# Moving GpSimd's low-part subtraction ahead of four row scatters, and holding two of the scatters until VectorE has divided

## The chip, the cores and the metric

The kernel runs on one core of a Trainium2 chip. The metric is the device time of one execution in microseconds (us), the median of several runs. The profile is of one execution, taken by the hardware profiler, with its own time beside it.

## What is computed

One transformer block in float32 on 4 sequences of 2048 tokens, 256 wide: a linear attention of 16 heads (cosformer), a layer norm, a mixture of 8 experts with 2 chosen for each token, a second layer norm.

```python
q, k = relu(x @ Wq.T + bq), relu(x @ Wk.T + bk);  v = x @ Wv.T + bv
q_ = concat([q * sin, q * cos]);  k_ = concat([k * sin, k * cos])      # by place in the sequence
kv = einsum('nld,nlm->ndm', k_, v)
z = 1.0 / maximum(einsum('nld,nd->nl', q_, k_.sum(axis=1)), EPS)
attn = einsum('nld,ndm->nlm', q_, kv) * z[:, :, None]
x = layernorm(x + attn @ Wo.T + bo)
topv, topi = top_k(x @ router_w.T, 2);  w = softmax(topv)
out = sum over the 2 chosen experts e of  w * (gelu(x @ w1[e].T) @ w2[e].T)
x = layernorm(x + out)
```

## The kernel before

The 8192 tokens are cut into 32 pairs of 128-token tiles (`NPAIR = 32`, 8 pairs to a sequence, `PB = 8`). Products are made in a reduced-precision format with both operands split into a high and a low part: ScalarE casts a pair's x to its high part (`xs<-xraw`, L823), and another engine subtracts it from x to give the low part (`x_low`). Up to pair 10 VectorE does that subtraction (L1028), from pair 11 on GpSimd does (`XLO_POOL = 11`, L1576).

There are two stages. In the first (to about 325 us) every engine runs a program of its own with a step for each pair, called `rep` in the code; the function `pipeline` writes some steps out and puts others in hardware loops. In step `rep`, keys, values and queries are made for pair `rep`, while attention is computed for the pair `LAG = 9` before it (`j = rep - 9`), the output projection and row statistics for `j - 1`, routing for `j - 2`, and the scatter of finished rows for `j - 3`. So the scatters start in step 12. In the second stage the experts run in 135 steps over gathered blocks of 128 rows, and the remaining pairs' attention is spread between them.

Every engine works through its own instructions in program order; semaphores tie them together. The order written out in the code is the order on the engine. What matters here, in step `rep`:

- VectorE: add the sine part of attention for the first tile (L1047), choose two experts for `j - 2` (`choose`: L1108 to L1125; L1115 compares and L1125 multiplies by the deviation, both from two inputs in SBUF), place columns (L1038), add the sine part of the second tile (L1047), then `normalise_attention`: clip the denominators (`den`, L1054, 128x32), reciprocal (L1056), multiply (L1058, which counts `at_ready`). Then the residual of `j - 1` (L1150), the sum of logits (L1091), the low part of a query (L1185), the gates of `j - 2` (up to L1141), the statistics of `j - 1` (the last is `mv`, L1164) and the low part of attention. In steps 16 and 24 `state_out` and `state_split` for a sequence that ended come in as well, `state_out` ahead of `choose`.
- GpSimd: four scatters of finished rows, each an indirect DMA (L1586, `expert_rows<-rows,idx`), `x_low` for pair `rep + 1` between the second and the third, then `half_deviation` (L1617 to L1622), which turns `mv` of `j - 1` into the scale and shift that ScalarE's `normalise` (L860) and VectorE's L1125 use in the next step.
- TensorE: among others, the rank products (L641, which wait for `choose` and for both L1047), the query products (L613), then the transposes of attention (L600), which wait for `at_ready` and for the logits' sum L1091 of this step, since that frees their bank.
- ScalarE: the cosine part (`tcos`, L831) ahead of each L1047, the high part of x (L823), `normalise` (L860), which writes into `rows` and so waits for the four scatters of the step before to have landed.
- SyncE: issues the loads; the load of the next x waits for `x_low` (L429), and the first gather of the second stage (L458) waits for the scatters of the first 20 pairs, the last four of which are those of step 31.

`hold(pool)` is a no-operation that stands behind waits.

Of the kernel before, what the change touches and what calls it, by code (L numbers as in the profile page):

```python
# [42 lines left out]
NPAIR = T // PAIR  # L43
# [65 lines left out]
def build(nc, x, xT, WqT, bq, WkT, bk, WvT, bv, WoT, Wo, bo, bo_columns, rwT, w1T, w2T, consts, out):  # L109
# [4 lines left out]
    with ctx:  # L114
# [3 lines left out]
        def sem(name):  # L118
            return ctx.enter_context(nc.semaphore(name))
# [168 lines left out]
        comb_step, at_ready, tlo_ready, qlo_ready = sem("comb_step"), sem("at_ready"), sem("tlo_ready"), sem("qlo_ready")  # L288
# [13 lines left out]
        XLO_POOL = PB + 3  # L302
# [40 lines left out]
        def hook(s):  # L343

            d, n = divmod(s - FIRST_GROUP, GROUP)
            return (GROUP_PAIRS + d, n) if FIRST_GROUP <= s < LAST_GROUP else (None, s - LAST_GROUP)
# [20 lines left out]
        def hold(eng):  # L367


            eng.nop(nofuse=True)  # L370

        def parts(rep):


            return (LAG <= rep, LAG < rep, LAG + 1 < rep, rep % PB == 0 and PB <= rep, PB <= rep)

        def lagged(u, rep):

            slot = (rep - LAG) % 2
            return u * 2 + (rep % 2 - LAG), u + (rep % 2 - LAG - slot) // 2  # L380
# [1177 lines left out]
        def _(pool):  # L1558
# [14 lines left out]
            def x_low(i, rep):  # L1573
                pool.wait_ge(xhi_ready, i + 1)
                hold(pool)
                nc.gpsimd.tensor_tensor(xs[:, rep % 2, 1], xraw[:, rep % 2], xs[:, rep % 2, 0].bitcast(F32), ALU.subtract)\  # L1576
                    .then_inc(xlo_late, 1)

            def scattered(jj):
                pool.wait_ge(pos_step, (jj + 1) * POS)  # L1580
                pool.wait_ge(route_step, (jj + 1) * ROUTE)
                pool.wait_ge(x1_ready, jj + 1)
                hold(pool)

            def scatter(slot, h, k):
                nc.gpsimd.indirect_dma_start(ex, bass.IndirectOffsetOnAxis(ap=idx[:, slot, h, k:k + 1], axis=0),  # L1586
                                             rows[:, slot, h, k, :], None).then_inc(s_rows[slot], 16)
# [12 lines left out]
            def weight_half(n):  # L1600

                e, kind = n // 2, n % 2
                pool.wait_ge(s_wraw[kind], e * 16 + 16)
                c0 = kind * HALF
                w_hi, w_lo = (w[:, e, part, c0:c0 + HALF] for part in range(2))
                nc.gpsimd.tensor_copy(w_hi, wraw[:, kind]).then_inc(wprep, 1)
                pool.wait_ge(wprep, 2 * n + 1)
                for c in range(0, HALF, D):
                    a = nc.gpsimd.tensor_tensor(w_lo[:, c:c + D], wraw[:, kind, c:c + D], w_hi[:, c:c + D].bitcast(F32),
                                                ALU.subtract)  # L1610
                a.then_inc(wprep, 1)

            def half_deviation(j):

                pool.wait_ge(norm_step, j * NORM + NORM_MV)
                hold(pool)
                nc.gpsimd.tensor_scalar(vare[:], mv[:, :, 1], 4.0, 4.0 * LN_EPS, ALU.mult, ALU.add).then_inc(pow_step, 1)  # L1617
                nc.gpsimd.tensor_scalar(shift1[:], mv[:, :, 0], -1.0, None, ALU.mult).then_inc(pow_step, 1)
                pool.wait_ge(pow_step, j * POW + 2)
                nc.gpsimd.tensor_tensor(rstd[:], vare[:], half_neg[:, 0:2], ALU.pow).then_inc(pow_step, 1)  # L1620
                pool.wait_ge(pow_step, j * POW + 3)
                nc.gpsimd.tensor_tensor(shift1[:], shift1[:], rstd[:], ALU.mult).then_inc(pow_step, 1)  # L1622

            def step(u, rep):
                attn, onward, route, _, _ = parts(rep)
                par = rep % 2
                i = u * 2 + par
                j, _ = lagged(u, rep)
                slot = (rep - LAG) % 2
                scatters = rep > LAG + 2  # L1630
                if scatters:
                    scattered(j - 3)
                    scatter(1 - slot, 0, 0)
                    scatter(1 - slot, 0, 1)
                if XLO_POOL <= rep + 1 < NPAIR:
                    x_low(i + 1, rep + 1)
                if scatters:
                    scatter(1 - slot, 1, 0)
                    scatter(1 - slot, 1, 1)
                if onward:  # L1640
                    half_deviation(j - 1)
                if rep == LAST_HALF_AT:
                    weight_half(HALVES - 1)
                if rep == NPAIR - 1:
                    late_weight()
                    scattered(j - 2)
                    for h in range(2):
                        for k in range(TOPK):
                            scatter(slot, h, k)

            pool.wait_ge(proj_low, 5)
            for n in range(HALVES - 1):
                weight_half(n)
            pipeline(pool, step, begin=PB, unrolled=PB)


# [27 lines left out]
            for s in range(STEPS):  # L1684
# [4 lines left out]
                j, n = hook(s)  # L1689
# [68 lines left out]
```

## Time and profile before

| | |
|---|---|
| median of 3 runs | 869.43 us (869.2 to 871.21) |
| the profiled execution's own time | 865.97 us |
| its span, first to last instruction | 864.2 us |
| granted TensorE clock, mean | 0.980 |
| busy: TensorE / VectorE / ScalarE / GpSimd | 800.2 (93%) / 576.6 (67%) / 460.9 (53%) / 424.9 (49%) us |
| steps 12 to 30 | about 104 to 306 us |

The span lies 1.8 us below the execution's time and 5.2 us below the median of the runs. Steps of the first stage are some 10 to 11 us long. Shares of busy time are averages over both stages; what a change in the first stage brings must be read from the waits of that stage.

### The profile page before, as it was taken

Reading aid. Unit: us, or ns where it says so; the run is one execution under the profiler, and the core shown is the slowest. Engines: PE = TensorE matmul, PEld = TensorE weight load, DVE = VectorE, ACT = ScalarE, POOL = GpSimd, SP = SyncE. Lnnn points to the kernel's source line nnn. Section 1 sums busy time; section 2 is a strip of 40 time slices with the busy share of each in tenths; the row PEclk is TensorE's granted clock in tenths of the full one; section 3 lists DMA queues with packets and bytes.
Section 4 is the critical chain, followed back from the end, with each engine's and each line's share of the span. In section 5 each row is a group of like instructions: output and inputs, shape, how many; then the busy total and the mean of one; then the engine's idle time right before and its main releaser. Section 6 shows DMA issues by size and latency. Waiting matters only on the chain.

```text
span 864.2 us, 22025 instructions
## 1 busy us (share of the span) xinstructions
PE 800.2 (93%) x6684; PEld 735.2 (85%) x6684; DVE 576.6 (67%) x1816; ACT 460.9 (53%) x1044; POOL 424.9 (49%) x545
## 2 busy tenths in 40 slices
PE   4998998999989976999999999999999999999990
PEld 4888988888889865999999999998999999999980
DVE  3335888888878885677666667665444467777773
ACT  4565766666667644444455444443444445656653
POOL 3885566566656654544454445453322224444442
PEclk9999999999999997999999999999999999999995
DMA  6453133233323324323333332232422255666644
GB/s 201 155 167 102 42 102 112 75 104 105 110 75 108 113 84 123 113 83 100 104 101 95 104 94 82 84 114 80 125 75 86 83 212 196 221 228 221 220 166 171
DMA packets 56468, 106.64 MB, mean 123 GB/s; under 512 B 9261, under 2 KB 37551, under 8 KB 54448
## 3 DMA queue, kind: packets, MB, share of 16 engines
q1 hardware_dynamic: 41296, 63.25, 24.7%
q0 software_dynamic: 12624, 33.84, 10.7%
q10 hardware_dynamic: 2448, 8.26, 2.6%
q8 instruction: 58, 0.95, 0.5%
q14 instruction: 42, 0.34, 0.1%
HBM read 61.91 MB, written 44.32 MB: 123 GB/s over the span
## 4 chain that ended last, share of the span: by engine, by line
PE 77%; DVE 10%; ACT 4%; issue 4%; DMA 2%; SPq 1%; DVEq 0%; POOL 0%; ACTq 0%; POOLq 0%
PE PS L736 22%; PE PS L724 22%; PE PS L540 11%; PE PS L754 7%; PE PS L577 4%; PE PS L713 3%; DVE den L1054 2%; PE PS L629 2%; PE PS L613 2%; PE PS L600 2%; DVE o L1047 1%; ACT tcos L831 1%; DVE xtok L1150 1%; DMA xraw<-in_xT 1%; ACT vs L851 1%
## 5 line engine op out<-in xcount | busy, mean ns | idle before, releaser
L1669 POOL DMA_INDIRECT token_rows<-xg x135 | 134.8, 998 | 280.5 <-DVE xg L1403 255.2
L736 PEld LDWEIGHTS PS<-w,hT 128*128 128x128 f32 x1620 | 211.6, 189 | 12.0 <-issue 1.8
L724 PE MATMUL PS<-w,xgT 128*128 x810 | 221.8, 409 | 0.0
L736 PE MATMUL PS<-w,hT 128*128 x1620 | 217.3, 283 | 0.8 <-ACT hT L994 0.8
L724 PEld LDWEIGHTS PS<-w,xgT 128*128 128x128 f32 x810 | 143.0, 190 | 24.2
L994 ACT ACTIVATE hT<-PS 128x512 fp32r<-128x512 f32 x135 | 80.8, 598 | 135.3 <-PE PS L754 135.3
L1586 POOL DMA_INDIRECT expert_rows<-rows,idx x128 | 126.9, 991 | 44.6 <-issue 32.9
L990 ACT ACTIVATE hg<-PS 128x512 f32<-128x512 f32 x135 | 80.6, 597 | 121.2 <-PE PS L724 120.9
L1468 DVE TENSOR_TENSOR hT<-PS,hT 128x512 fp32r<-128x512 f32 x135 | 93.4, 692 | 75.2 <-ACT hT L994 75.2
L1395 DVE TENSOR_TENSOR xgT<-PS,xgT 128x256 fp32r<-128x256 f32 x135 | 57.0, 422 | 78.2 <-ACT xgT L960 77.0
L754 PE MATMUL PS<-cst,hg 128*128 128x128 f32 x540 | 81.0, 272 | 0.7 <-ACT hg L990 0.7
L540 PE MATMUL PS<-wk,xs 128*128 128x264 f32 x384 | 65.4, 307 | 13.8 <-DVE wv L1333 8.3
L1403 DVE SCALAR_TENSOR_TENSOR xg<-PS,xg 128x256 f32<-128x256 f32 x135 | 65.1, 482 | 14.0 <-PE PS L736 4.5
L540 PEld LDWEIGHTS PS<-wk,xs 128*128 128x128 f32 x384 | 52.1, 195 | 21.2 <-ACT vs L851 10.0
L577 PE MATMUL PS<-sts,qs 128*128 128x272 f32 x384 | 62.1, 298 | 7.1 <-DVE o L1047 2.4
L754 PEld LDWEIGHTS PS<-cst,hg 128*128 128x128 f32 x540 | 62.6, 140 | 1.4 <-ACT hg L990 1.4
L577 PEld LDWEIGHTS PS<-sts,qs 128*128 128x128 f32 x384 | 52.3, 192 | 9.0 <-issue 5.7
L713 PE MATMUL PS<-cst,xg 128*128 128x128 f32 x270 | 52.3, 276 | 6.4 <-DMA xg<-expert_rows 5.3
L613 PE MATMUL PS<-xs,wq 128*128 128x256 f32 x384 | 57.5, 296 | 0.0
L540 PE MATMUL PS<-wv,xs 128*128 128x256 f32 x384 | 57.1, 286 | 0.0
L629 PE MATMUL PS<-wo,aT 128*128 128x264 f32 x384 | 56.7, 286 | 0.0
L1047 DVE SCALAR_TENSOR_TENSOR o<-PS,cst,tcos 128x272 f32<-128x272 f32 x64 | 32.0, 501 | 30.9 <-ACT tcos L831 30.7
(179 smaller groups left out, 1302.1 us busy)
## 6 DMA issues: line engine op xcount, KB each, us to landing
xg<-expert_rows SPq DMA_DIRECT2D x135, 130.0 KB, 2.1
z<-token_rows SPq DMA_DIRECT2D x15, 1024.0 KB, 7.4
xraw<-in_xT SPq DMA_DIRECT2D x32, 256.0 KB, 3.3
xtok<-in_x SPq DMA_DIRECT2D x32, 256.0 KB, 3.1
out_y<-z ACTq DMA_DIRECT2D x15, 512.0 KB, 3.6
wraw<-in_w1T SPq DMA_DIRECT2D x7, 512.0 KB, 3.7
wraw<-in_w2T SPq DMA_DIRECT2D x7, 512.0 KB, 3.8
token_rows<-xg POOLq DMA_INDIRECT x135, 2.8
```

The lines of the kernel that those rows point to most:

```text
L540: return nc.tensor.matmul(PS[:, bank, 0:columns], xs[:, rep % 2, a, k, h * P:(h + 1) * P], weights[:, b, k, :], start=(n == 0), stop=(n == ...
L577: mm = nc.tensor.matmul(PS[:, bN + half, 0:2 * NW], qs[:, a, half, h * P:(h + 1) * P], sts[:, b, half].rearrange("p a b -> p (a b)"), star ...
L613: mm = nc.tensor.matmul(PS[:, bQ, half * PAIR:(half + 1) * PAIR], wq[:, a, k, half * P:(half + 1) * P], xs[:, rep % 2, b, k, :], start=(n ...
L713: mm = nc.tensor.transpose(PS[:, gX, k * P:(k + 1) * P], xg[:, XG_SLOTS[s % NXG], k * P:(k + 1) * P], ident)
L724: mm = nc.tensor.matmul(PS[:, gH, :], xgT[:, s % 2, a, k, :], w[:, bass.ds(e, 1), b, k * F:(k + 1) * F].rearrange("p o f -> p (o f)"), sta ...
L736: return nc.tensor.matmul(PS[:, gY, 0:D], hT[:, a, k, :], w[:, bass.ds(e, 1), b, HALF + k * D:HALF + (k + 1) * D] .rearrange("p o f -> p ( ...
L754: mm = nc.tensor.transpose(PS[:, gT, k * P:(k + 1) * P], hg[:, k * P:(k + 1) * P], ident)
L990: nc.scalar.activation(hg[:], PS[:, gH, :], ACT.Gelu, scale=2.0).then_inc(gelu_ready, 1)
L994: nc.scalar.activation(hT[:, 0].rearrange("p k t -> p (k t)"), PS[:, gT, :], ACT.Copy)\
L1468: nc.vector.tensor_tensor(hT[:, 1].rearrange("p k t -> p (k t)"), PS[:, gT, :], hT[:, 0].rearrange("p k t -> p (k t)").bitcast(F32), ALU.s ...
L1586: nc.gpsimd.indirect_dma_start(ex, bass.IndirectOffsetOnAxis(ap=idx[:, slot, h, k:k + 1], axis=0), rows[:, slot, h, k, :], None).then_inc( ...
L1669: nc.gpsimd.indirect_dma_start(yd, bass.IndirectOffsetOnAxis(ap=xg[:, XG_SLOTS[s % NXG], C_DST:C_GATE].bitcast(U32), axis=0), xg[:, XG_SLO ...
```

## The change

In GpSimd's step, `x_low` is moved ahead of the waits and the four scatters, and the third scatter gets a wait of its own: for `at_ready` of the step's own pair `j`, that is for VectorE's L1058 in the same step.

```diff
                 scatters = rep > LAG + 2
+                if XLO_POOL <= rep + 1 < NPAIR:
+                    x_low(i + 1, rep + 1)
                 if scatters:
                     scattered(j - 3)
                     scatter(1 - slot, 0, 0)
                     scatter(1 - slot, 0, 1)
-                if XLO_POOL <= rep + 1 < NPAIR:
-                    x_low(i + 1, rep + 1)
-                if scatters:
+                    pool.wait_ge(at_ready, j + 1)
+                    hold(pool)
                     scatter(1 - slot, 1, 0)
                     scatter(1 - slot, 1, 1)
```

The instructions of TensorE, VectorE, ScalarE and SyncE keep their order. On GpSimd, step 30 of the kernel before reads so (L1586 are scatters, L1576 is `x_low`, the rest `half_deviation`):

```order
L1586 DMA expert_rows<-rows,idx 66688x260 [waits x1_ready,pos_step,route_step]
L1586 DMA expert_rows<-rows,idx 66688x260
L1576 TENSOR_TENSOR xs<-xraw,xs 128x512 [waits xhi_ready]
L1586 DMA expert_rows<-rows,idx 66688x260 x2
L1617 TENSOR_SCALAR vare<-mv 128x2 [waits norm_step]
L1618 TENSOR_SCALAR shift<-mv 128x2
L1620 TENSOR_TENSOR rstd<-vare,half_neg 128x2 [waits pow_step]
L1622 TENSOR_TENSOR shift<-shift,rstd 128x2 [waits pow_step]
```

The same step of the changed kernel:

```order
L1576 TENSOR_TENSOR xs<-xraw,xs 128x512 [waits xhi_ready]
L1586 DMA expert_rows<-rows,idx 66688x260 [waits x1_ready,pos_step,route_step]
L1586 DMA expert_rows<-rows,idx 66688x260
L1586 DMA expert_rows<-rows,idx 66688x260 [waits at_ready]
L1586 DMA expert_rows<-rows,idx 66688x260
L1617 TENSOR_SCALAR vare<-mv 128x2 [waits norm_step]
L1618 TENSOR_SCALAR shift<-mv 128x2
L1620 TENSOR_TENSOR rstd<-vare,half_neg 128x2 [waits pow_step]
```

The subtraction has moved in front of the first two scatters, and the third scatter now waits for `at_ready`. It is the same in steps 12 to 30. Step 31 has no `x_low`; before, its four scatters run through:

```order
L1586 DMA expert_rows<-rows,idx 66688x260 [waits x1_ready,pos_step,route_step]
L1586 DMA expert_rows<-rows,idx 66688x260 x3
L1617 TENSOR_SCALAR vare<-mv 128x2 [waits norm_step]
L1618 TENSOR_SCALAR shift<-mv 128x2
L1620 TENSOR_TENSOR rstd<-vare,half_neg 128x2 [waits pow_step]
```

In the changed kernel the second half of them has the wait too:

```order
L1586 DMA expert_rows<-rows,idx 66688x260 [waits x1_ready,pos_step,route_step]
L1586 DMA expert_rows<-rows,idx 66688x260
L1586 DMA expert_rows<-rows,idx 66688x260 [waits at_ready]
L1586 DMA expert_rows<-rows,idx 66688x260
L1617 TENSOR_SCALAR vare<-mv 128x2 [waits norm_step]
```

Only the wait is new there; nothing is moved.

## Rows read from the trace of the kernel before

**Rows 1.** The page's chain that ended last, by line

```profile
PE PS L736 22%; PE PS L724 22%; PE PS L540 11%; PE PS L754 7%; PE PS L577 4%; PE PS L713 3%; DVE den L1054 2%; PE PS L629 2%; PE PS L613 2%; PE PS L600 2%; DVE o L1047 1%; ACT tcos L831 1%; DVE xtok L1150 1%; DMA xraw<-in_xT 1%; ACT vs L851 1%
```

**Rows 2.** TensorE's waits, 104 to 306 us: total us, times, longest

```profile
PE PS L600 <- DVE lsum L1091: 8.3, 15, 1.0
PE PS L641 <- DVE o L1047: 3.0, 2, 1.5
PE PS L691 <- DVE rows L1141: 0.6, 1, 0.6
```

**Rows 3.** Timeline of steps 26 and 27: start, duration, engine, line [idle before]

```profile
260.26 0.87 DVE L1054 TENSOR_SCALAR den<-o 128x32 f32<-128x32 f32 x1
...
266.72 0.66 ACT L823 ACTIVATE xs<-xraw 128x512 fp32r<-128x512 f32 x1
...
268.05 0.19 DVE L1115 TENSOR_TENSOR oh<-cst,ix 128x32 f32<-128x32 f32 x1
...
268.66 0.16 DVE L1125 TENSOR_TENSOR dls<-dl,rstd 128x2 f32<-128x2 f32 x1
...
269.14 0.49 ACT L831 ACTIVATE tcos<-PS,cst 128x272 f32<-128x272 f32 x1 [0.36 <-PE PS L577]
...
269.66 0.50 DVE L1047 SCALAR_TENSOR_TENSOR o<-PS,cst,tcos 128x272 f32<-128x272 f32 x1 [0.75 <-ACT tcos L831]
...
270.07 1.31 POOL L1576 TENSOR_TENSOR xs<-xraw,xs 128x512 fp32r<-128x512 f32 x1
...
270.20 1.23 DVE L1054 TENSOR_SCALAR den<-o 128x32 f32<-128x32 f32 x1
...
271.85 0.69 DVE L1058 TENSOR_TENSOR o<-o,den 128x512 f32<-128x512 f32 x1
...
272.84 0.96 POOL L1586 DMA_INDIRECT expert_rows<-rows,idx  x1 [0.30 <-issue]
...
273.38 0.63 PE L600 MATMUL PS<-cst,o 128*128 128x128 f32 x4 [0.39 <-DVE lsum L1091]
...
275.83 0.23 POOL L1617 TENSOR_SCALAR vare<-mv 128x2 f32<-128x2 f32 x1 [2.03 <-DVE mv L1164]
...
277.55 1.54 ACT L860 ACTIVATE rows<-xtok,shift,rstd 128x512 f32<-128x512 f32 x2
```

**Rows 4.** VectorE's L1054, grouped: 104 to 306 us, then 330 to 550 us

```profile
L1054 DVE TENSOR_SCALAR den<-o 128x32 f32<-128x32 f32 x19 | 20.9, 1098 | 0.7
...
L1054 DVE TENSOR_SCALAR den<-o 128x32 f32<-128x32 f32 x9 | 1.6, 181 | 0.3
```

**Rows 5.** Timeline of step 24, where state_out comes ahead of choose

```profile
235.72 1.79 DVE L1125 TENSOR_TENSOR dls<-dl,rstd 128x2 f32<-128x2 f32 x1
...
236.19 1.29 POOL L1576 TENSOR_TENSOR xs<-xraw,xs 128x512 fp32r<-128x512 f32 x1
...
237.65 0.98 POOL L1586 DMA_INDIRECT expert_rows<-rows,idx  x1 [0.17 <-issue]
...
238.03 0.18 DVE L1054 TENSOR_SCALAR den<-o 128x32 f32<-128x32 f32 x1
```

**Rows 6.** Busy time in two steps: length, PE, PEld, DVE, ACT, POOL, clock

```profile
258.73:268.66 9.93, 9.77 (x109) 9.12 (x108) 8.22 (x34) 6.98 (x19) 6.49 (x9) 1.00 0.36 109
268.66:278.98 10.32, 9.82 (x109) 9.15 (x108) 8.57 (x35) 6.99 (x19) 6.57 (x10) 1.00 0.33 104
```

**Rows 7.** The scatters, 104 to 306 us: durations in ns, and us to landing

```profile
L1586 POOL DMA_INDIRECT expert_rows<-rows,idx x76: 956/985/1223, 104.7 to 304.0; - x76
...
DMA to landing us min/median/max: 2.4/2.9/4.7
```

**Rows 8.** Timeline of step 31 and the first gather of stage two

```profile
314.67 0.69 DVE L1058 TENSOR_TENSOR o<-o,den 128x512 f32<-128x512 f32 x1
...
318.82 0.24 POOL L1617 TENSOR_SCALAR vare<-mv 128x2 f32<-128x2 f32 x1 [4.65 <-DVE mv L1164]
...
324.08 17.16 SPq L458 DMA_DIRECT2D xg<-expert_rows  x6
```

## The prediction, made before the changed kernel had run

> **What bounds the kernel now.** I read the page first. TensorE is busy for 93% of the span, and the chain that ended last runs over its matmuls; the first entry of another engine is VectorE's `den`, L1054, with 2% [rows 1], some 17 us of 864.2. That is much for an instruction on 128x32 numbers, so I looked at it alone. Its 19 executions of steps 12 to 30 take 1098 ns on average, while 9 of the same shape in the second stage take 181 ns [rows 4]. The timeline of step 27 shows why: L1054 begins at 270.20, 0.13 us after GpSimd's `x_low` (L1576, 270.07 to 271.38), and ends at 271.43, 0.05 after it [rows 3]. In step 24 L1125 meets the same `x_low` instead: 1.79 us where it takes 0.16 in step 27; it ends at 237.51 with `x_low` at 237.48, and L1054, now behind it, takes 0.18 [rows 3, 5]. So a GpSimd subtraction that reads SBUF blocks these VectorE instructions until it is over.
>
> Then TensorE's waits, since it sets the end. In steps 12 to 30 it waits 15 times, 8.3 us in all, at the transposes L600 for VectorE's L1091, which stands three instructions behind L1054; twice, 3.0 us, at the rank products L641, which is `choose` held up in steps 16 and 24; and once, 0.6 us, in step 30 for L1141, which is further down the same VectorE queue [rows 2]. These 11.9 us are what the collision costs TensorE, not the 17 us: the query products run while VectorE is blocked. Step 26 shows the floor: L1054 takes 0.87 us there, TensorE has no wait at L600 in that step, and the stretch takes 9.93 us, 9.77 of it busy; the next, with L1054 at 1.23 and the wait at 0.39, takes 10.32 [rows 3, 6]. The wait is what exceeds 1.23 - 0.39 = 0.84 us, so with L1054 at 0.18 VectorE has 0.66 us to spare at L600.
>
> **The change part by part.** *`x_low` ahead of the scatters.* It can start when ScalarE's cast of x is over: 266.72 + 0.66 = 267.38 in step 27. `half_deviation` of the step before is done by then: it is over before L860 begins, which comes right behind the cast on ScalarE. With 0.15 us for the semaphore I place `x_low` at 267.53 to 268.84, 2.54 us earlier than now. L1054 at 270.20 then meets no subtraction: 1.23 becomes 0.18, 1.05 us less.
>
> What it meets instead: L1115 starts at 268.05, has two SBUF inputs like L1125, and will be blocked to 268.84 + 0.05 = 268.89 instead of ending at 268.24, 0.65 us. The rest of `choose` moves with it. But VectorE is idle for 0.75 us before L1047, waiting for ScalarE's `tcos` [rows 3]; 0.65 fits, so L1047 and L1054 don't move. Cost 0; without that idle time 0.65 us a step, and even that VectorE has to spare at L600 (0.66). The bounds: 0 if L1115 isn't blocked, 1.3 us (the whole subtraction) at most, of which 1.3 - 0.75 = 0.55 would come through, still under 0.66.
>
> In steps 16 and 24 `choose` is later because `state_out` comes first. Shifted by the same 2.54, `x_low` of step 24 runs from 233.65 to 234.94. L1115 starts 0.61 before L1125 [rows 3], at 235.11: it's free, L1125 takes 0.16 instead of 1.79, and L641's wait goes, which is 1.5 us at the longest [rows 2]. Both steps: -3.0 us. Step 30's wait of 0.6 behind L1141: VectorE comes 1.05 us earlier or more, TensorE by its wait at L600, some 0.5 us, and the difference covers the 0.6: -0.6.
>
> *The scatters behind `x_low`.* The first starts 0.17 to 0.6 us behind it (the gap now behind `x_low`, and the one ahead of a step's first scatter), so at 269.0 to 269.4, and two take 2.3 us (1.07 + 0.30 + 0.96): to 271.4 or 271.8. They now lie beside L1054 and L1056. Does a scatter block these? In step 24 L1054 ran inside a scatter (237.65 to 238.63) in 0.18 us [rows 5], and the nine of the second stage lie between scatters and took 181 ns [rows 4]. I take 0; the upper bound is a scatter's 1.0 us a step (second rival).
>
> By the Trainium skill (SBUF, section Who interferes with whom), a tensor_scalar in a two-port mode and a GpSimd instruction exclude each other, and one with two SBUF inputs is held up only by a GpSimd instruction that reads SBUF. The long L1054 and L1125 agree. Descriptor writing should hold L1054 up by the first half of that rule; the 0.18 us inside a scatter speaks against it here. By the rule the new place beside the scatters would give back what `x_low` released; that is the second rival.
>
> *The wait for `at_ready`.* It is reached at 271.4 to 271.8. L1058 now ends at 272.54; 1.05 earlier is 271.49. So the third scatter starts at about 271.7 to 271.9 and the fourth is over 2.3 us later, 274.0 to 274.2, against 273.80 now. Queued behind the wait are the two scatters, `half_deviation`, the next `x_low` and the next scatters; ScalarE's `normalise`, VectorE's L1125 and TensorE's next keys wait for them. `half_deviation` waits for `mv` anyway: L1617 at 275.83 after 2.03 us idle [rows 3], in the new order 1.05 earlier, 274.78. GpSimd is free 0.6 us before that: cost 0. L860 waits for the fourth scatter to land: it starts 4.71 us after it now (277.55 - 272.84), and 4.71 - 0.4 (started later) - 0.4 (shorter step) = 3.9 then, over a median landing of 2.9 and below the longest, 4.7 [rows 3, 7]. ScalarE may wait in a step or two: 0 to 0.8 us each.
>
> *Step 31.* The wait holds the last two scatters until L1058 has ended at 315.36; they are over by about 317.9, before L1617 at 318.82, and landed by 317.9 - 0.96 + 4.7 = 321.6 at worst, before the first gather at 324.08 [rows 7, 8]. Cost 0. Without that cover the gather would be late by as much, and TensorE with it.
>
> Sum: -8.3 - 3.0 - 0.6 = **-11.9 us**. The profiled execution would go from 865.97 to 854.1. Its time is 3.5 us below the median of the runs, 869.43; I carry the difference over to the median: **857.5 us**.
>
> **The rivals.**
>
> *First: part comes back through ScalarE.* If the fourth scatter lands late in many steps (more than 3.9 us after its start), `normalise` and the `tcos` behind it are late, and up to 0.4 us a step is lost: 19 x 0.4 = 7.6 at most, some 5 likely: 862.5 us. For it: the longest landing of 4.7 us. Against: the median of 2.9.
>
> *Second: the stall stays.* If any GpSimd work, scatters included, blocks L1054 or L1056 when it starts at the right moment, the two scatters beside them take the place of `x_low`, and the 15 waits stay. Only steps 16 and 24 gain, 3.0 us: 866.4 us. For it: L1054 now meets a different phase of a scatter than in step 24. Against: rows 4 and 5. This is also the case in which the change doesn't do what it is for.
>
> *Third: slower, by the wait for `at_ready`.* GpSimd becomes a link in the ring: `at_ready`, two scatters, `half_deviation`, `normalise`, `tcos`, L1047 and `at_ready` again. The ring has 0.6 us to spare at L1617 and 0.4 us at `tcos`, which waits 0.36 us for TensorE [rows 3]. Each us beyond 1.0 costs 19 us. To take back the 11.9 and 2.6 more it must be 14.5 / 19 = 0.76 beyond, so the scatters behind the wait would have to end 1.8 us later than I have them: 873 us with a little more. The longest of 76 scatters, 1.22 us, is 0.26 above the usual [rows 7]; two of them add 0.5. For it speaks only that the four scatters, `x_low` and `half_deviation` now share a step with a fixed point in its middle.
>
> **How the numbers follow.** A measurement of this kernel tells about 0.3% from no change, 2.6 us. The forecast of 857.5 has 0.77, the first rival 0.07, the second 0.10, the third 0.06. Of the second I count 0.06 within 0.3% (its 3.0 us are at the bound) and 0.04 faster; of the third 0.02 within, 0.04 slower; the first is faster. So faster 0.88, same 0.08, slower 0.04. The likeliest case alone reaches from 855 (the small waits of TensorE and a later floor gain another 2 us) to 861 (3 us of delays that I took as hidden). The range goes up to the first rival: **854.5 to 864.0**, which leaves out most of the second and third.
>
> **What would show it.** In the profile of the changed kernel: L1054 at about 0.18 us in all of steps 12 to 30; `x_low` ending before L1047 of the second tile; L1115 at about 0.8 us instead of 0.19 in most steps and 0.19 in steps 16 and 24; the waits at L600 and L641 gone; a short idle time of VectorE still before the second L1047; GpSimd still idle before L1617, by under 1 us instead of 2; steps of about 9.9 us; the second stage the same, begun 12 us earlier. The prediction is wrong if L1054 or L1056 stays above 0.5 us (second rival), if L1617 follows the fourth scatter without idle time and TensorE waits at L577 for `tcos` and L1047 (third), or if L860 waits for scatters (first). It is wrong too if VectorE's delay in `choose` reaches TensorE by a way that I haven't priced.

## The result and the profile after

The changed kernel takes **857.47 us** (median of 4 runs, 857.12 to 858.07) against 869.6 of the kernel before (4 runs, 869.2 to 871.21): a ratio of 0.9868, 95% interval 0.9854 to 0.9881. In two later sets of runs, each beside its own runs of the kernel before, it was 0.9877 (0.9856 to 0.9898) and 0.9851 (0.9824 to 0.9877). The forecast was 857.5. The total is right, but two of its terms are wrong and offset each other, so the agreement to the last digit is luck. The experiments below show where.

The profiled execution took 858.07 us, span 856.3. The page's chain that ended last, by line, for the changed kernel:

```profile
PE PS L736 23%; PE PS L724 22%; PE PS L540 10%; PE PS L754 7%; PE PS L577 4%; PE PS L713 4%; PE PS L613 4%; PE PS L629 3%; PE PS L600 1%; PE PS L560 1%; ACT vs L851 1%; DMA boc<-in_bo_columns 1%; ACT vs L850 1%; PE PS L547 1%; DVE o L1047 1%
```

L1054, the first entry of another engine in [rows 1], is gone from it. The groups of VectorE's instructions from 104 to 300 us (total us, mean ns, idle before) say what became of it, to be read against [rows 4]:

```profile
L1115 DVE TENSOR_TENSOR oh<-cst,ix 128x32 f32<-128x32 f32 x20 | 13.4, 672 | 0.7
L1054 DVE TENSOR_SCALAR den<-o 128x32 f32<-128x32 f32 x19 | 3.8, 200 | 0.7
```

L1054 went from 1098 to 200 ns. L1115, which took 0.19 us [rows 3], is blocked in its place, 672 ns on average. TensorE's waits from 104 to 306 us, which answer to [rows 2]:

```profile
PE PS L540 <- ACT vs L851: 3.5, 15, 0.4
...
PE PS L641 <- DVE o L1047: 2.4, 4, 1.1
PE PS L691 <- DVE rows L1141: 0.6, 1, 0.6
PE PS L600 <- DVE lsum L1091: 0.4, 1, 0.4
```

At L600 0.4 us is left of 8.3. At L641 the waits have not gone: 4 of them, 2.4 us, instead of 2, 3.0 us; and L540 waits 3.5 us for ScalarE, where it waited 0.6 before. The timeline of step 27 (start, duration, engine, line, idle time before and what ended it; "issue" means that the profile shows nothing that ended it) is the counterpart of [rows 3]. Here and below, rows of other instructions between those shown are left out:

```profile
257.27 1.30 POOL L1576 TENSOR_TENSOR xs<-xraw,xs 128x512 fp32r<-128x512 f32 x1 [0.69 <-ACT xs L823]
257.80 0.82 DVE L1115 TENSOR_TENSOR oh<-cst,ix 128x32 f32<-128x32 f32 x1
...
259.42 0.50 DVE L1047 SCALAR_TENSOR_TENSOR o<-PS,cst,tcos 128x272 f32<-128x272 f32 x1
259.95 0.18 DVE L1054 TENSOR_SCALAR den<-o 128x32 f32<-128x32 f32 x1
...
260.56 0.69 DVE L1058 TENSOR_TENSOR o<-o,den 128x512 f32<-128x512 f32 x1
261.85 0.68 DVE L1185 TENSOR_TENSOR qs<-q,qs 128x512 fp32r<-128x512 f32 x1
262.03 1.33 POOL L1586 DMA_INDIRECT expert_rows<-rows,idx  x1 [0.96 <-issue]
...
263.67 0.96 POOL L1586 DMA_INDIRECT expert_rows<-rows,idx  x1 [0.31 <-issue]
264.21 0.15 DVE L1164 BATCH_NORM_AGGREGATE mv<-stats 128x2 f32<-128x6 f32 x1
264.69 0.20 POOL L1617 TENSOR_SCALAR vare<-mv 128x2 f32<-128x2 f32 x1
```

`x_low` lies where the prediction put it, and L1115 takes 0.82 us beside it. L1047 begins 0.03 us after `tcos` has ended (at 259.39), as it did before [rows 3], so the delay of L1115 is covered, and L1054 comes on time. But the third scatter begins 0.78 us after L1058 has ended (261.25 to 262.03) and takes 1.33 us, not 0.96. It and the fourth are over at 264.63, after `mv` (264.36), so L1617 follows with no idle time; GpSimd had 2.03 us there before [rows 3]. Of the 20 steps from 12 to 31, 12 have none; the others have 0.65 to 0.76 us, and steps 16 and 24 have 1.81.

The stretch from the end of step 11 (the end of L1622) to the first gather of the second stage, in busy time of each engine (length, PE, PEld, DVE, ACT, POOL, clock). First the kernel before:

```profile
103.75:324.08 220.33, 200.27 (x2141) 185.57 (x2140) 184.24 (x728) 141.14 (x358) 135.70 (x184) 0.98 0.31 98
```

Then the changed kernel, a step without late waits ahead of the stretch:

```profile
252.87:262.57 9.70, 9.54 (x109) 9.06 (x108) 8.16 (x36) 6.97 (x18) 6.96 (x10) 1.00 0.33 111
...
104.40:313.22 208.82, 195.32 (x2142) 183.45 (x2140) 173.79 (x728) 140.77 (x358) 139.71 (x185) 0.99 0.32 104
```

220.3 us became 208.8, 11.5 us less. What lies outside the stretch is 864.2 - 220.3 = 543.9 us before and 856.3 - 208.8 = 547.5 after. Later profiles have 543.0 for the kernel before and 543.3 and 544.8 for the changed kernel, so most of those 3.6 us is the spread of executions, and I don't explain them. They are also why the two profiled spans differ by 7.9 us and the medians by 12.1. And one step of the changed kernel takes 9.70 us where the floor was read as 9.93 [rows 6].

The granted clock differs between the two stretches, 0.98 and 0.99, and it matters little. In the kernel before it is 0.87 in steps 16 and 25. In a later profile of the same program (the copy in part 3) it is 1.00 in both: step 16 takes 13.06 us instead of 13.07, with TensorE busy for 9.97 instead of 11.55, and step 25 takes 10.34 instead of 10.66, with 9.64 busy instead of 10.50. The lower clock filled idle time and cost some 0.3 us; that stretch is 220.00 us instead of 220.33.

### The profile page after: what moved, and what is told of

The parts are those of the page before. It is cut to its first block, busy times and chain, and to the rows that moved or that the text cites. A ratio compares the mean times of both kernels' runs of the same rounds, so it can differ in the third digit from the quotient of the medians.

```text
span 856.3 us, 22053 instructions
## 1 busy us (share of the span) xinstructions
PE 800.6 (93%) x6684; PEld 736.7 (86%) x6684; DVE 566.9 (66%) x1816; ACT 460.2 (54%) x1044; POOL 428.8 (50%) x545
## 3 DMA queue, kind: packets, MB, share of 16 engines
q0 software_dynamic: 12624, 33.84, 10.8%
## 4 chain that ended last, share of the span: by engine, by line
PE 80%; DVE 6%; issue 5%; ACT 5%; DMA 3%; SPq 1%; POOL 1%; ACTq 0%; POOLq 0%; DVEq 0%
PE PS L736 23%; PE PS L724 22%; PE PS L540 10%; PE PS L754 7%; PE PS L577 4%; PE PS L713 4%; PE PS L613 4%; PE PS L629 3%; PE PS L600 1%; PE PS L560 1%; ACT vs L851 1%; DMA boc<-in_bo_columns 1%; ACT vs L850 1%; PE PS L547 1%; DVE o L1047 1%
## 5 line engine op out<-in xcount | busy, mean ns | idle before, releaser
L1586 POOL DMA_INDIRECT expert_rows<-rows,idx x128 | 131.0, 1024 | 60.1 <-issue 35.4
L540 PE MATMUL PS<-wk,xs 128*128 128x264 f32 x384 | 65.0, 306 | 15.0 <-DVE wv L1333 8.3
L540 PEld LDWEIGHTS PS<-wk,xs 128*128 128x128 f32 x384 | 52.0, 194 | 22.3 <-ACT vs L851 12.5
L540 PE MATMUL PS<-wv,xs 128*128 128x256 f32 x384 | 57.0, 285 | 0.0
L713 PE MATMUL PS<-cst,xg 128*128 128x128 f32 x270 | 52.6, 277 | 4.3 <-DMA xg<-expert_rows 4.2
L860 ACT ACTIVATE rows<-xtok,shift,rstd 128x512 f32<-128x512 f32 x64 | 48.8, 818 | 8.9 <-DMA expert_rows<-rows,idx 6.3
```

The costliest lines, as they stand in the source:

```text
L540: return nc.tensor.matmul(PS[:, bank, 0:columns], xs[:, rep % 2, a, k, h * P:(h + 1) * P], weights[:, b, k, :], start=(n == 0), stop=(n == ...
L713: mm = nc.tensor.transpose(PS[:, gX, k * P:(k + 1) * P], xg[:, XG_SLOTS[s % NXG], k * P:(k + 1) * P], ident)
```

## The experiments

After the measurement above the runs came in four sets, called 1 to 4. The kernels of one set ran on the same chip beside the same runs of the kernel before. They are compared within a set only; part 3 shows why. An expected time is to be read against the kernel before as known when it was written: 869.6 us for the runs of set 1.

### 1. The change in halves (set 1)

The kernel before took 865.5 us here (15 runs, 863.08 to 867.03).

**The move alone**, against the kernel before:

```diff
+                if XLO_POOL <= rep + 1 < NPAIR:
+                    x_low(i + 1, rep + 1)
                 if scatters:
                     scattered(j - 3)
                     scatter(1 - slot, 0, 0)
                     scatter(1 - slot, 0, 1)
-                if XLO_POOL <= rep + 1 < NPAIR:
-                    x_low(i + 1, rep + 1)
-                if scatters:
                     scatter(1 - slot, 1, 0)
                     scatter(1 - slot, 1, 1)
```

> x_low moved ahead of the four scatters, and no wait for at_ready. My theory: the gain is all from the move, since the subtraction no longer meets L1054, and the wait for at_ready only costs: in the changed kernel the third scatter starts 0.8 us after L1058 and takes 1.3, so the fourth starts 0.8 us later than before and lands too late for ScalarE's normalise in 5 steps (6.3 us of idle time there, of which 2.4 us reach TensorE at L641). Without the wait these are gone: about 855 us, 2 to 4 us under the changed kernel, no wait of L860 for scatters, L1054 at 0.18 us. Rival: the wait keeps scatters off the divide chain, and without it L1054, L1056 or L1058 gets longer by up to 1 us a step: 860 us or more.

Measured: 848.96 us (5 runs), ratio 0.9813 (0.9794 to 0.9832), the fastest of all. The timeline of one of its steps:

```profile
264.25 0.18 DVE L1054 TENSOR_SCALAR den<-o 128x32 f32<-128x32 f32 x1
264.40 0.96 POOL L1586 DMA_INDIRECT expert_rows<-rows,idx  x1 [0.30 <-issue]
264.85 0.69 DVE L1058 TENSOR_TENSOR o<-o,den 128x512 f32<-128x512 f32 x1
265.67 0.96 POOL L1586 DMA_INDIRECT expert_rows<-rows,idx  x1 [0.30 <-issue]
...
268.82 0.23 POOL L1617 TENSOR_SCALAR vare<-mv 128x2 f32<-128x2 f32 x1 [0.92 <-DVE mv L1164]
```

The scatters run through at 0.96 us each beside L1054, L1056 and L1058; L1054 takes 0.18 (187 ns on average), and GpSimd has 0.92 us to spare ahead of L1617. One of its steps and its stretch:

```profile
266.85:276.56 9.71, 9.55 (x109) 9.07 (x108) 8.16 (x36) 6.97 (x18) 6.62 (x9) 1.00 0.32 111
...
102.26:305.27 203.01, 192.03 (x2142) 181.42 (x2140) 173.41 (x728) 140.62 (x358) 134.82 (x184) 1.00 0.33 107
```

The stretch is 220.33 - 203.01 = 17.3 us shorter than before, not 11.9, and most of its steps take 9.5 to 9.8 us. By the medians of the set the kernel is 16.5 us faster. So the move is worth some 17 us, and the hold takes part of it back.

**The hold alone**: `x_low` stays in its old place, and the third scatter waits for `at_ready`.

```diff
                 if scatters:
+                    pool.wait_ge(at_ready, j + 1)
+                    hold(pool)
                     scatter(1 - slot, 1, 0)
                     scatter(1 - slot, 1, 1)
```

> x_low stays between the second and third scatter, the wait for at_ready is added. My theory: the collision stays, L1054 at about 1.1 us, the waits at L600 stay at about 8 us and those at L641 in steps 16 and 24 too; the later scatters make normalise late in a few steps besides: 870 to 876 us, slower than the kernel before by 0 to 6 us. Rival (the wait is what gains): 860 us or less.

Measured: 869.21 us (10 runs), ratio 1.004 (1.0027 to 1.0052), so 3.7 us slower than before. TensorE's waits at L600 and L641 (104 to 306 us), and the collision of one step:

```profile
PE PS L600 <- DVE lsum L1091: 8.3, 13, 1.0
PE PS L641 <- DVE o L1047: 6.2, 7, 1.6
...
274.52 0.69 DVE L1058 TENSOR_TENSOR o<-o,den 128x512 f32<-128x512 f32 x1
275.81 0.69 DVE L1185 TENSOR_TENSOR qs<-q,qs 128x512 fp32r<-128x512 f32 x1
276.00 1.35 POOL L1586 DMA_INDIRECT expert_rows<-rows,idx  x1 [1.95 <-DVE o L1058]
```

L600's waits are those of before; those at L641 rose from 3.0 to 6.2 us. Here, too, the held scatter starts 0.79 us behind L1058 and takes 1.35 us. L1054 keeps its 1001 ns. So the hold removes nothing by itself and costs something in either order.

**The changed kernel again**, in the same set:

> The changed kernel itself, on the same chip and in the same rounds as the others, as their yardstick: 857 to 858.5 us. A second profile of it also tells whether the 3 us by which the second stage was longer in the first profile than in the one of the kernel before belong to the change: if they do, the stage from the first gather to the end takes 543 us again; if it is the spread of executions, it lies anywhere from 539 to 543.

Measured: 854.46 us (4 runs), ratio 0.9877 (0.9856 to 0.9898), a stretch of 206.2 us. Against the move alone in this set that is 5.5 us more by the medians and 206.2 - 203.0 = 3.2 by the stretch; but the profile was taken in the fastest of the four runs, 851.31 us, and the others took 854.3 to 855.7. Between the profile shown above and the move alone it is 208.8 - 203.0 = 5.8. The cost of the hold is therefore 3 to 6 us, by two profiles and one pair of medians.

How it comes about is in the changed kernel's step 30 (the profile shown above):

```profile
288.89 1.52 ACT L860 ACTIVATE rows<-xtok,shift,rstd 128x512 f32<-128x512 f32 x2 [1.98 <-DMA expert_rows<-rows,idx]
...
290.81 0.50 DVE L1047 SCALAR_TENSOR_TENSOR o<-PS,cst,tcos 128x272 f32<-128x272 f32 x1 [1.73 <-ACT tcos L831]
...
291.46 0.17 PE L641 MATMUL PS<-chosen,ones_bf 128*128 128x8 bf16 x1 [1.13 <-DVE o L1047]
...
293.43 1.33 POOL L1586 DMA_INDIRECT expert_rows<-rows,idx  x1 [2.58 <-DVE o L1058]
```

The rows are one chain. L860 waits 1.98 us for the held scatters to land, `tcos` is late behind it, L1047 waits 1.73 us for `tcos`, and TensorE waits 1.13 us at L641 for VectorE. L1058 is late as well, and so are the next held scatters. ScalarE has 5 such waits at L860, 6.3 us in all; the move alone has none. That is the first rival's mechanism, and it reaches TensorE at L641. Read by TensorE's weight loads, which wait longer than its matmuls, L641 has 3.2 us of waits in the changed kernel and 2.9 in its copy of this set, and the move alone has none. That is the part of the 3 to 6 us that the traces locate; the rest isn't located.

**`x_low` in two halves, in its old place**, without a hold:

```diff
-                nc.gpsimd.tensor_tensor(xs[:, rep % 2, 1], xraw[:, rep % 2], xs[:, rep % 2, 0].bitcast(F32), ALU.subtract)\
-                    .then_inc(xlo_late, 1)
+                for k in range(KD):
+                    a = nc.gpsimd.tensor_tensor(xs[:, rep % 2, 1, k], xraw[:, rep % 2, k], xs[:, rep % 2, 0, k].bitcast(F32),
+                                                ALU.subtract)
+                a.then_inc(xlo_late, 1)
```

> The kernel before with x_low in its old place, but as two GpSimd instructions of 128x256 in place of one of 128x512. Theory: the VectorE instruction is blocked until the GpSimd instruction that runs is over, so L1054 is blocked to the end of the first half (about 0.7 us after x_low's start) or, if GpSimd's second half gets in first, to the end of both. If it is let in between: L1054 at 0.6 to 0.8 us, no waits at L600 (a reserve of 0.84 us), about 860 us. If GpSimd keeps the way for both halves: no change, 869 to 870 us.

Measured: 854.65 us (4 runs), ratio 0.9871 (0.9851 to 0.9892): as much as the whole change, without moving anything. One collision in its timeline:

```profile
261.93 1.43 POOL L1577 TENSOR_TENSOR xs<-xraw,xs 128x256 fp32r<-128x256 f32 x2
262.05 0.72 DVE L1054 TENSOR_SCALAR den<-o 128x32 f32<-128x32 f32 x1
```

L1054 ends at 262.77, 0.59 us before the pair of halves does (263.36): it gets in between them. Its mean is 433 ns. So the block lasts as long as one GpSimd instruction, not as long as a series of them. I had expected 0.6 to 0.8 us there.

### 2. Where the hold and the subtraction may stand (set 2)

The kernel before took 869.95 us here (7 runs). Four kernels, each with `x_low` moved. The first two cuts are against the move alone. First, with the wait ahead of the fourth scatter alone,

```diff
                     scatter(1 - slot, 1, 0)
+                    pool.wait_ge(at_ready, j + 1)
+                    hold(pool)
                     scatter(1 - slot, 1, 1)
```

> x_low first as in the changed kernel, but the wait for at_ready stands before the fourth scatter only. The third scatter begins before L1058 is over or right at its end, so the wait itself takes next to nothing. Theory (what costs is that the scatter behind the wait begins 0.8 us after it is released, not overlapped with the one before, and so lands later): a delay of the fourth scatter by 0.3 to 0.5 us against the kernel with the move alone, L860 waits for it in no or one step, time 849 to 852 us, between the move alone (849.0) and the changed kernel (854.5), nearer to the first. Rival (keeping scatters off the divide chain costs by itself, wherever the wait is): as the changed kernel, 854 us.

with the wait ahead of all four,

```diff
                     scattered(j - 3)
+                    pool.wait_ge(at_ready, j + 1)
+                    hold(pool)
                     scatter(1 - slot, 0, 0)
```

> x_low first, the wait for at_ready before all four scatters. Theory (my third rival's ring: at_ready, scatters, half_deviation, normalise, tcos, L1047): four scatters end 0.8 + 1.35 + 3 x 1.3 = 6 us after L1058, mv is ready 3.2 us after it, so half_deviation is 2.8 us late; with a reserve of 0.4 us at tcos some 2.4 us a step come through, 19 steps: 45 us, some 895 us; less where the fourth scatter's landing is later still: up to 910. If GpSimd's queue had slack that I don't see: under 870.

with the subtraction behind all four scatters and no wait (against the kernel before),

```diff
                     scatter(1 - slot, 0, 0)
                     scatter(1 - slot, 0, 1)
+                    scatter(1 - slot, 1, 0)
+                    scatter(1 - slot, 1, 1)
                 if XLO_POOL <= rep + 1 < NPAIR:
                     x_low(i + 1, rep + 1)
-                if scatters:
-                    scatter(1 - slot, 1, 0)
-                    scatter(1 - slot, 1, 1)
```

> No hold, and x_low behind all four scatters. Theory (the subtraction blocks whichever VectorE instruction with two SBUF inputs or of L1054's kind comes first, and it matters whom it meets): it now runs some 2.5 us later than in the kernel before, beside the residual, L1185 and the gates, behind TensorE's release at L600: L1054 at 0.18, waits at L600 gone, L1185 or one of L1135 to L1141 longer by up to 1.2 us instead, which makes mv and half_deviation late; and TensorE's next keys wait for x_low by 0 to 0.5 us a step. 852 to 862 us. Rival (the early place is what gains, the collision with L1054 is not the cause): 866 us or more.

and the move alone with the subtraction in two halves, cut as in set 1:

> The move alone, with x_low as two instructions of 128x256. Theory: where x_low is now, the stall of L1115 is already covered by VectorE's idle time before L1047, so a shorter stall brings nothing: the same as the move alone, 848 to 851 us, L1115 at 0.3 to 0.8. If that stall were on TensorE's path after all: 2 us or more below it.

Measured: 876.42, 887.58, 885.27 and 876.93 us, ratios 1.0082 (1.0064 to 1.0101), 1.021 (1.0192 to 1.0228), 1.0167 (1.015 to 1.0184) and 1.0092 (1.0069 to 1.0114). I had expected the first and the last near the move alone, well below the kernel before. Both missed by about 3%, and so did the third, expected at 852 to 862 us. The second came out below the 895 to 910 expected. Part 3 is about why. All four have pauses of TensorE that part 3 describes, and these may hide or add small differences. Compared with each other they still say three things.

With all four held, TensorE's and ScalarE's waits (104 to 306 us) are

```profile
PE PS L641 <- DVE o L1047: 16.7, 13, 2.5
...
ACT rows L860 <- POOL shift L1622: 22.5, 12, 2.6
```

16.7 us at L641 instead of 2.4, and `half_deviation` (L1622) is late for L860 in 12 steps. This is the third rival's ring, closed on purpose: GpSimd has four scatters and `half_deviation` behind the fixed point, where the changed kernel has two. It costs 11.2 us over the kernel with the fourth held, although it has hardly any of the pauses that part 3 shows for the other. Its granted clock is lower, 0.85 in six of the steps to 30, but that isn't what makes it slow: step 26 takes 11.49 us at 0.85, and step 29 takes 11.50 at 1.00.

With the subtraction last, the timeline of one step:

```profile
267.42 2.44 DVE L1185 TENSOR_TENSOR qs<-q,qs 128x512 fp32r<-128x512 f32 x1
268.02 1.28 POOL L1576 TENSOR_TENSOR xs<-xraw,xs 128x512 fp32r<-128x512 f32 x1
```

L1054 is free (187 ns), and L1185, two SBUF inputs, takes the collision: 1641 ns on average instead of 680. It was under way for 0.6 us when `x_low` began, and took 1.76 us more than it does alone, longer than the whole subtraction. The place decides what is hit. Of the three places tried, L1115 is the cheapest to hit, because VectorE idles behind it. How much time the last place costs by this alone isn't shown: of the 10.8 us by which its stretch is longer than that of the kernel with the fourth held (240.4 against 229.6), 4.8 lie in steps 23 and 24, where its granted clock was 0.88 and 0.89.

With the move and two halves, L1115 takes 222 ns, where it takes 694 in the kernel with the fourth held, and the time does not follow (876.93 against 876.42). That agrees with the start of L1047 right behind `tcos` in the changed kernel: L1115's 0.5 us cost nothing, as the prediction had it. By times alone it is shown only among kernels with pauses.

### 3. The same programs in other sets (sets 3 and 4)

In set 3 (kernel before: 869.46 us, 9 runs) the move alone and the kernel with the fourth scatter held ran again, word for word.

> The move alone once more, beside the kernel that holds the fourth scatter. In the last set all four kernels had a pause of TensorE of about 1 us in most steps, which waits for nothing that the profile shows, in the midst of matmuls; no kernel of the sets before had it. Theory A, the pauses come with the circumstances of a set of runs (loading, placing, neighbours): the move alone now may have them too, 870 us or more, or the other kernel has lost them. Theory B, they come with the program: the move alone has none, 847 to 851 us beside 864 to 867 of the kernel before, or 851 to 855 beside 870.

> The same program as before with the fourth scatter held. Theory A (circumstances): without pauses it takes 850 to 854 us, 0 to 4 us over the move alone of this set. Theory B (program): 875 us again, with TensorE's pauses in nearly every step.

Measured: the move alone 876.46 us (5 runs, 875.43 to 881.04), ratio 1.0084 (1.0054 to 1.0113), where the same program had 848.96 and 0.9813 in set 1. The kernel with the fourth held: 876.08 us (5 runs), 1.0077 (1.0054 to 1.01), as in set 2. So a kernel without those edits can be as slow, and what kept set 2's kernels slow was most likely not their edits. Beside the pauses, holding the fourth scatter costs nothing measurable over the move alone (0.4 us less by the medians of one set). TensorE's waits in the move alone of set 3 (104 to 306 us), then a step of its timeline:

```profile
PE PS L540 <- issue: 9.1, 21, 0.8
...
PE PS L600 <- issue: 4.2, 9, 0.9
...
267.67 0.60 PE L600 MATMUL PS<-cst,o 128*128 128x128 f32 x4
268.03 0.86 PE L540 MATMUL PS<-wk,xs 128*128 128x264 f32 x5
269.62 0.28 PE L540 MATMUL PS<-wk,xs 128*128 128x264 f32 x1 [0.73 <-issue]
269.92 0.36 DVE L1099 SCALAR_TENSOR_TENSOR lg<-minus_sums,mv,lsum 128x8 f32<-128x8 f32 x2 [0.46 <-issue]
269.94 0.60 ACT L869 ACTIVATE aT<-PS 128x512 fp32r<-128x512 f32 x1 [3.77 <-remote]
```

TensorE stops for 0.73 us in the middle of a product of six matmuls, where nothing that the profile shows holds it ("issue"). ScalarE's L869 starts 1.67 us after L600 has ended by its record (268.27), where it was 0.04 in set 1. So either L600 was over later than its record has it, or ScalarE was late too; the profile doesn't tell. VectorE finishes the statistics meanwhile (the last, L1164, from 269.32 to 269.47), and then it is idle for 0.46 us ahead of L1099, in this step alone, with nothing named either. Such pauses come once or twice in most steps, in the first stage only, and most steps then take 10.8 us or more instead of 9.7; steps 17 and 25 take 9.1 as in set 1. The clock granted is 1.00 in all steps from 12 to 30 of this profile, so it is not the clock. All the kernels of sets 2 and 3 have them, though few with all four scatters held (L540 <- issue 3 times, 1.2 us); no profile of sets 1 and 4 does, and neither do the profiles of [rows 2] and of the result.

The last two runs were to see the kernel before and the changed kernel in one more set:

> The kernel before, word for word. Its time must be that of the kernel before in this set (ratio 1.000, within 0.3%). What is asked of its profile is whether TensorE has the pauses marked 'issue' in the first stage that the five kernels of the two sets before this one had (15 to 18 us in all at L540, L600 and L613). Theory A (the pauses come with the circumstances of a set, whatever the kernel): if this set has them, the kernel before has some 15 us of them too; its time stayed at 869.5 to 870 there against 865.5 in the set without them, so they would then have to be hidden behind its own waits for VectorE (11.9 us), and the stretch from L1622 of step 11 to the first gather is 220 to 226 us. Theory B (the pauses need TensorE to be fed without stops, as only the kernels with x_low first do): the kernel before shows under 2 us of them and a stretch of 219 to 223 us in every set.

> The changed kernel, word for word, beside the kernel before on the same chip. Theory A: in a set without pauses 0.987 again (854 to 859 us, a stretch of 206 to 209 us, no waits marked 'issue' of over 2 us in all); in a set with them 1.006 to 1.012 (875 to 880 us, a stretch near 229 us, 14 us or more of such waits), since the move alone went from 0.981 to 1.008 between such sets. Theory B, in the form that the wait which the changed kernel has ahead of its third scatter protects it: 0.985 to 0.990 in any set, while the move alone, which has no such wait, is the one that changes.

Measured (kernel before in the set: 865.48 us, 13 runs): the copy of the kernel before 866.06 us (10 runs), ratio 1.0004 (0.9991 to 1.0017); the changed kernel 854.12 us (4 runs), 0.9851 (0.9824 to 0.9877). TensorE's waits of the copy, 104 to 306 us:

```profile
PE PS L600 <- DVE lsum L1091: 9.3, 17, 1.0
```

L641 has 3.0 us in 2 waits beside it. They are those of [rows 2], and no pauses are among them; nor are there any in the changed kernel's. The set had none, so these runs don't tell the two theories apart. They do confirm the sizes: stretches of 220.0 and 209.0 us, 11.0 apart. Of the 209.0, some 1.5 us belong to the granted clock and not to the kernel: it is 0.87 in step 17, which takes 10.73 us, where the changed kernel takes 9.2 at 1.00 in the two other profiles.

**What stays open.** The cause of the pauses. They don't come with the program alone, since one program went from 848.96 to 876.46 us. Nor do they come with the chip alone: sets 1 and 2 ran on one chip, the first without pauses and the second with them, but with other programs. Sets 3 and 4 ran on two others, and the move alone was never run twice on one chip. So a cause in chip and program together isn't excluded. They may also depend on the program: each kernel that had them feeds TensorE without its waits at L600, and the kernel before, whose pauses were never looked for in such a set, rose only from 865.5 to about 870. The changed kernel was never run in sets 2 or 3, so whether its hold protects it, or it would have been slower than before there, isn't known. Its three ratios come with profiles without pauses, the first of them beside a kernel before at 869.6, so the level of the kernel before alone doesn't tell a set with pauses.

## Why the prediction was right

Point by point, by its own steps.

- **`x_low` blocks L1054 until it is over.** Right. L1054 fell to 200 ns when the subtraction was moved ahead of the scatters and to 187 when it was moved behind them, kept 1001 ns with the hold alone, and fell to 433 when the subtraction was cut in two in its place.
- **The move: -8.3 (L600), -3.0 (L641), -0.6 (L691), 11.9 in all.** The mechanism is right and the term too small: the move alone gives 17.3. Of this, 220.33 - 200.27 = 20.1 against 203.01 - 192.03 = 11.0 is idle time of TensorE, 9.1 us. The other 8.2 lie in what its records show as busy, 200.27 against 192.03. Some 2.4 of these are the lower clock in steps 16 and 25, which cost the stretch only 0.3; so the two shares don't say where the gain is. The step of the working that failed is "Step 26 shows the floor": it took 9.93 us with 9.77 busy, and most steps of the move alone take 9.71 with 9.55 busy. Step 26 had no wait at L600 in TensorE's matmul rows, but its rows of weight loads, which I didn't read, have one of 0.21 us there. Some 19 steps of 0.22 are 4.2 us of the 5.4 that were missing, by estimate. The waits of the weight loads in the kernel before, 104 to 306 us:

```profile
PEld PS L600 <- DVE o L1058: 5.8, 7, 1.2
PEld PS L600 <- issue: 5.3, 9, 0.7
...
PEld PS L641 <- DVE dls L1125: 3.3, 2, 1.7
```

  11.1 us at L600 instead of 8.3. With L641's 3.3 and 0.8 at L691 they would have given 15.2, nearer to the 17.3. It isn't an exact account: in the move alone other waits of the weight loads grew (L540 for ScalarE from 4.1 to 5.8 us), and the same window holds a later part of a faster kernel.
- **L1115 blocked by 0.65 instead, at no cost.** Right: 672 ns instead of 194, L1047 still begins as soon as `tcos` is there, and freeing L1115 again brought nothing.
- **Steps 16 and 24, and step 30.** Half right. In the move alone no wait at L641 or L691 is left among those of TensorE's matmuls (its weight loads have 0.4 us at L691). In the changed kernel 2.4 and 0.6 us stand there, but the 2.4 are other waits than those of before, made by the late landings.
- **The scatters beside L1054 and L1056 block nothing.** Right in size, and the second rival is out as the main effect: in the move alone L1054 took 0.18 us in 17 of the 19 steps and 0.25 in two, and L1056 0.35 in all. But a scatter can hold L1054 up. The changed kernel has one such row, in step 19:

```profile
178.17 0.96 POOL L1586 DMA_INDIRECT expert_rows<-rows,idx  x1 [0.30 <-issue]
...
178.73 0.38 DVE L1054 TENSOR_SCALAR den<-o 128x32 f32<-128x32 f32 x1
```

  L1054 begins 0.56 us into the scatter and ends 0.02 before it, at 0.38 us instead of 0.18. The two other profiles of the changed kernel have five more: beginning 0.55 to 0.61 us into a scatter, L1054 takes 0.33 to 0.40 and ends with the scatter each time. In step 24 of the kernel before it began 0.38 in, and was over before that part. So the phase counts, as the second rival had it, and the price is 0.2 us in one to three steps, not 1.0 in each. The Trainium skill (SBUF, section Who interferes with whom) has descriptor writing held apart from a tensor_scalar in a two-port mode; these six rows agree with it, and the many at 0.18 inside a scatter show that it isn't held for the whole of one.
- **The wait for `at_ready`, cost 0.** Wrong: 3 to 6 us. Two rows differ from the working. The third scatter begins 0.78 us after L1058, not 0.2 to 0.4, and takes 1.33, not 0.96; together some 0.8 us later than placed. That uses up the 0.6 of spare time at L1617 in 12 of 20 steps and leaves the fourth scatter less than the 3.9 us to land that I had worked out: 5 waits at L860 of up to 1.98 us, where I had one or two of up to 0.8. The first rival's mechanism was real, its sign (L860 waits for scatters) came, and it took 3 to 6 of the 7.6 us that it could. The longer scatter is VectorE's doing: the steps of the changed kernel come in two kinds, which these rows of step 13 and those of step 27 above show.

```profile
119.42 0.96 POOL L1586 DMA_INDIRECT expert_rows<-rows,idx  x1 [1.15 <-DVE o L1058]
119.42 0.72 DVE L1185 TENSOR_TENSOR qs<-q,qs 128x512 fp32r<-128x512 f32 x1
```

  In both the scatter begins 0.78 to 0.79 us after L1058. Where L1185, with two inputs in SBUF, has begun 0.18 us ahead of it, the scatter takes 1.33 (13 of the 19 steps 12 to 30); where L1185 begins with it or up to 0.17 after it, 0.95 to 0.96 (steps 13 to 15 and 21 to 23), and GpSimd keeps 0.65 us or more of idle time at L1617. In the kernel with the fourth scatter held, a scatter that ran on without a late start took 1.17 where L1185 had begun 0.34 us ahead of it. So it is the neighbour that lengthens it, and not the late start.
- **Step 31, cost 0.** Right in cost: the wait at L713 for the first gather did not grow (4.24 us, 5.33 before). But the spare time that was counted on is gone: L1617 follows the fourth scatter without idle time, where 4.65 us were idle before [rows 8].

```profile
306.98 0.96 POOL L1586 DMA_INDIRECT expert_rows<-rows,idx  x1 [0.30 <-issue]
...
315.84 0.44 PE L713 MATMUL PS<-cst,xg 128*128 128x128 f32 x1 [4.24 <-DMA xg<-expert_rows]
```

So 17.3 - 5.8 = 11.5 us in the stretch, where the forecast had 11.9 - 0. It is two errors of 5 to 6 us with opposite signs, and that they cancel is luck. The number alone would have let both pass; only the move without the hold showed their sizes. The third rival's ring exists (all four held: 11 us over the kernel with one held), but with two scatters it did not make the kernel slower than before.

## What to carry to other kernels

Where VectorE's small instructions take several times their usual duration, look for a GpSimd instruction on SBUF that ends when they do, and move it to where VectorE idles next, or cut it in two: here the move gave 1.9% and the cut 1.3%, each in the one set in which it ran without pauses of TensorE. Don't add an order between engines that nothing needs: the same move without its wait was 0.6% faster in the same set. Size a removed wait by the rows of TensorE's weight loads as well as those of the matmuls, and take as a floor only a step in which neither has one. And when kernels come out 3% from where they should in a second set of runs, repeat an unchanged program before you explain their edits.

## What the runs showed that was not expected

- TensorE's pauses, the longest of 0.8 to 1.1 us and one or two in most steps, in every kernel with `x_low` moved of two of the four sets; the same program took 27.5 us more with them.
- A scatter that a semaphore releases started 0.78 us behind the end of L1058 in the changed kernel and 0.79 with the hold alone. It took 1.33 to 1.35 us where L1185 was under way when it began, and 0.95 to 0.96 where L1185 began with it or after it, at the same late start.
- L1054 takes 0.33 to 0.40 us instead of 0.18 when it begins 0.55 to 0.61 us into a scatter, and ends with it (six rows in three profiles).
- A blocked VectorE instruction gets in between two GpSimd instructions that follow each other without a gap: 0.72 us in the row shown and 0.43 on average, instead of 1.1 on average.
- `x_low` beginning 0.6 us into L1185 made that take 2.44 us instead of 0.68: 1.76 more, longer than the 1.28 of the subtraction itself.
